# Expert stages of a six-stage kernel: on-chip slot inversion, a gather and a scatter per block, a norm by tile, shorter routing

## Chip, core and metric

One core of a Trainium2 chip runs the whole kernel in one launch. The metric is the device time of that core in microseconds (us), lower is better. Engines: PE (TensorE), DVE (VectorE), ACT (ScalarE), POOL (GpSimd), SP (SyncE, which issues DMAs).

## What is computed

x has 1024 tokens of 256 features. Six stages follow one another, "fafmsm": expert layer with 2 experts (f), attention (a), f again, expert layer with 8 experts (m), a state-space mixer (s), m again. Each starts with a layer norm of x and adds its result to x.

```python
x = x + 0.5 * _L0_ffn_ref(_layernorm(x), ...)   # 2 experts, the best one counts
x = x + _L0_attn_ref(_layernorm(x), ...)
x = x + 0.5 * _L0_ffn_ref(_layernorm(x), ...)
x = x + 0.5 * _L1_ffn_ref(_layernorm(x), ...)   # 8 experts, the best two count
x = x + _L1_attn_ref(_layernorm(x), ...)        # mixer
x = x + 0.5 * _L1_ffn_ref(_layernorm(x), ...)

# f: probs = softmax(x @ gate_w.T); sel = argmax; y = (silu(x Wg) * (x Wu)) Wd of expert sel, times probs[sel]
# m: probs = softmax(gelu(x @ rw1) @ rw2); top 2; for each expert e and rank k:
#      Ye = gelu(x w1[e] + b1[e]) w2[e] + b2[e];  Ce = gelu(b1[e]) w2[e] + b2[e]
#      out += active * wgt[k] * (Ye where idx[k] == e, else Ce)
```

## The kernel before

**Tiles.** x stays in SBUF as 8 tiles of 128 tokens (X). Matrices are held as two float16 parts (high and low), and a product is three matmuls: high by high, high by low, low by high.

**An expert stage** (`moe_stage`, stages 1, 3, 4, 6) has these steps.
- Norm (`layernorm_stage`): DVE waits for all of x, then runs statistics (L121), aggregation (L124), epsilon (L126), the root on ACT (L142), reciprocal (L128) and the normalised rows XN (L130), each for all eight tiles. Then PE turns each tile (L153), ACT makes the high half XTh (L145), DVE the low half XTl (L134), two PSUM banks in turn.
- Router: PE (L362; L373 and L378 with 8 experts), DVE from L551 on: softmax, masks, rank by rank.
- Slots: tokens are sorted by expert into blocks of 128 rows. PE counts (L387, L390), DVE computes a slot for each token (L578 to L591) and the expert of each block (L593 to L596).
- Rows: POOL scatters the rows of XN to their slots in DRAM (L683, one indirect DMA for each tile and rank: 8 with one expert a token, 16 with two). SP then loads whole blocks (L704).
- With 8 experts, DVE also makes coefficients (L600 to L611), PE turns them (L398), ACT copies them (L506); in stage 4 the bias product follows (L777, 192 matmuls; L794 on DVE).
- Blocks: NB0 = 9 with 2 experts, NB1 = 23 with 8. In step b PE runs turn_h(b) (L441), first(b+1) (L430), turn_x(b+2) (L412) and second(b) (L457). DVE copies the result (L640), SP stores it (L708). SP's order is load(b+3), store(b).
- Return: once all blocks are stored, POOL gathers each token's rows (L694), four buffers, and DVE adds them to X (L666), and with 8 experts the bias part (L671).

**Other stages.** Attention (stage 2) has its own norm and adds its result at L1206, in the order of tiles 0, 4, 1, 5 and so on. The mixer (stage 5) loads constants by SP once x is there, DVE starts with L1674, and adds its result at L1738. Each engine's program is the stages' programs one after another, so an engine reaches the next stage only when it has issued all of this one.

**Weights.** In stage 1 three matrices are split in two halves by ACT (L259) and DVE (L264), then the attention weights (L191, L201). POOL splits the matrix w1 in 17 chunks (L216, L201), 14 of them between its scatters and its gathers of stage 1, the other 3 at the start of attention. Then it splits w2 in 20 chunks to DRAM (L1226, L1228). Stage 4 loads w2 back (L760, 8 MB), stage 6 again.

Of the kernel before, what the change touches and what calls it, by code (L numbers as in the profile page):

```python
# [19 lines left out]
P = 128  # L20
# [14 lines left out]
EPS = 1e-5  # L35

# [69 lines left out]
def layernorm_stage(c, x_done, x_count, XN):  # L106

    s_var = c.sem("ln_var", 1)
    s_sd = c.sem("ln_sd", 1)
# [5 lines left out]
    stats, mv, veps, sd, rstd = c.ln_stats, c.ln_mv, c.ln_veps, c.ln_sd, c.ln_rstd  # L115

    def dve(eng):
        link = c.dve_link
        eng.wait_ge(*x_done(x_count))
        for t in range(NT):  # L120
            ins = eng.bn_stats(stats[:, t, :], X[:, t, :])  # L121
        link(ins)
        for t in range(NT):
            ins = eng.bn_aggr(mv[:, t, :], stats[:, t, :])  # L124
        link(ins)
        eng.tensor_scalar(veps[:, :], mv[:, :, 1], EPS, None, ALU.add).then_inc(s_var.sem, 1)  # L126
        eng.wait_ge(*s_sd(1))
        link(eng.reciprocal(rstd[:, :], sd[:, :]))  # L128
        for t in range(NT):
            eng.tensor_scalar(XN[:, t, :], X[:, t, :], mv[:, t, 0:1], rstd[:, t:t + 1],  # L130
                              ALU.subtract, ALU.mult).then_inc(s_xn.sem, 1)
        for t in range(NT):
            eng.wait_ge(*s_hi(t + 1))
            eng.tensor_tensor(XTl[:, :, t * P:(t + 1) * P], pst(t), XTh[:, :, t * P:(t + 1) * P],  # L134
                              ALU.subtract).then_inc(s_lo.sem, 1)

    def pst(t):
        return c.bank(6 + t % 2)[:, 0:D].rearrange("p (k t) -> p k t", k=KD)

    def act(eng):  # L140
        eng.wait_ge(*s_var(1))
        eng.activation(sd[:, :], veps[:, :], ACT.Sqrt).then_inc(s_sd.sem, 1)  # L142
        for t in range(NT):
            eng.wait_ge(*s_tps(t + 1))
            eng.activation(XTh[:, :, t * P:(t + 1) * P], pst(t), ACT.Copy).then_inc(s_hi.sem, 1)  # L145

    def pe(eng):
        for t in range(NT):
            eng.wait_ge(*s_xn(t + 1))
            if t >= 2:  # L150
                eng.wait_ge(*s_lo(t - 1))
            for k in range(KD):
                ins = eng.transpose(pst(t)[:, k, :], XN[:, t, k * P:(k + 1) * P], c.ident[:, :])  # L153
            ins.then_inc(s_tps.sem, 1)
# [1933 lines left out]
```

## Time and profile before

| | us |
|---|---|
| median of 3 runs (lowest, highest) | 1248.28 (1246.53, 1250.77) |
| profiled execution, own time | 1248.47 |
| its span, first to last instruction | 1246.9 |
| PE busy | 910.6 (73%) |
| DVE, ACT, POOL busy | 558.5, 350.2, 383.0 |

The page gives busy time by engine, the chain of work that ended last, and groups of instructions by line. A "granted clock" is TensorE's, as a share of full speed. In the timeline a row has the start in us, the duration in us, the engine, the line, the operation, output <- input, the count and, in brackets, how long the engine was idle before it and what ended that.

### The profile page before, as it was taken

To read this page: it belongs to the slowest core of one execution; us is meant where nothing else is said; L and a number is where in the kernel's file an instruction comes from. 1 tells how busy PE (TensorE), PEld (TensorE's weight loads), DVE (VectorE), ACT (ScalarE), POOL (GpSimd) and SP (SyncE) were. 2 spreads that over 40 slices of the span, in tenths; PEclk is the share of its full clock that TensorE was granted. 3 is DMA by queue.
4 is the path that set the end of the run, shared out by engine and by line. 5 is a ranking of instruction groups with operands and counts; after the bars stand their busy time and mean duration, and the time that the engine had idled before them with its cause. 6 is when DMAs were issued, how large, how long until landed. Compare 5 with 4: busy or idle time off the path is not lost.

```text
span 1246.9 us, 18377 instructions
## 1 busy us (share of the span) xinstructions
PE 910.6 (73%) x5986; PEld 516.2 (41%) x5987; DVE 558.5 (45%) x1090; ACT 350.2 (28%) x594; POOL 383.0 (31%) x360
## 2 busy tenths in 40 slices
PE   2199625498887279924899999568699744999993
PEld 1056412122223136612556666334244431666661
DVE  5523373567772423354023333365699550332333
ACT  3322111155553122211033333136211221333330
POOL 0695167888100100033100000413798313000004
PEclk9999957599998579965899999769999966999996
DMA  8453127555100010053101111230000152111103
GB/s 306 149 150 93 37 83 239 186 172 180 52 15 2 22 38 26 22 198 155 43 27 34 42 34 34 65 125 1 1 0 1 34 251 70 34 38 37 34 30 106
DMA packets 47576, 98.63 MB, mean 79 GB/s; under 512 B 10208, under 2 KB 32240, under 8 KB 46624
## 3 DMA queue, kind: packets, MB, share of 16 engines
q1 hardware_dynamic: 36400, 57.09, 13.1%
q0 software_dynamic: 11120, 40.77, 10.4%
q8 instruction: 38, 0.62, 0.2%
q14 instruction: 18, 0.15, 0.0%
HBM read 65.97 MB, written 31.85 MB: 78 GB/s over the span
## 4 chain that ended last, share of the span: by engine, by line
PE 65%; DVE 13%; issue 6%; DMA 5%; POOL 5%; ACT 3%; SPq 2%; DVEq 0%; POOLq 0%; ACTq 0%
PE psum L430 19%; PE psum L457 14%; PE psum L1057 6%; PE psum L441 4%; POOL xg_dram L683 3%; PE psum L1515 3%; PE psum L425 2%; POOL mem L694 2%; PE psum L777 2%; PE psum L1032 2%; DVE mem L130 2%; DVE mem L1151 1%; PE psum L1462 1%; PE psum L412 1%; DMA mem<-yg_dram,mem 1%
## 5 line engine op out<-in xcount | busy, mean ns | idle before, releaser
L430 PE MATMUL psum<-mem 128*128 x984 | 240.8, 391 | 0.4 <-issue 0.3
L694 POOL DMA_INDIRECT mem<-yg_dram,mem x48 | 46.0, 958 | 514.8 <-DMA yg_dram<-mem 501.4
L457 PE MATMUL psum<-mem 128*128 x1536 | 178.2, 273 | 4.7 <-DVE mem L632 4.7
L457 PEld LDWEIGHTS psum<-mem 128*128 128x128 f16 x1536 | 149.9, 98 | 23.3 <-issue 5.6
L430 PEld LDWEIGHTS psum<-mem 128*128 128x128 f16 x984 | 90.9, 100 | 119.2 <-issue 33.9
L683 POOL DMA_INDIRECT xg_dram<-mem x48 | 56.6, 1180 | 211.5 <-DVE mem L591 198.1
L1151 DVE TENSOR_REDUCE mem<-psum 128x2 f32<-128x1024 f32 (+2 forms) x96 | 89.4, 951 | 59.5 <-PE psum L1010 37.6
L1109 ACT ACTIVATE mem<-psum 128x512 f32<-128x512 f32 (+1 forms) x160 | 80.0, 552 | 106.2 <-PE psum L1040 66.2
L632 DVE TENSOR_TENSOR mem<-psum,mem 128x512 f16<-128x512 f32 x128 | 82.5, 686 | 49.8 <-ACT mem L525 49.8
L525 ACT ACTIVATE mem<-psum 128x512 f16<-128x512 f32 x128 | 69.5, 595 | 124.4 <-PE psum L441 124.4
L153 PE MATMUL psum<-ident,mem 128*128 128x128 f32 x96 | 26.8, 430 | 97.3 <-DVE mem L130 78.0
L1057 PE MATMUL psum<-mem 128*17 128x512 f32 (+3 forms) x384 | 81.5, 521 | 17.2 <-DVE mem L1170 17.2
L620 DVE COPY mem<-mem 16x128 f16 (+1 forms) x46 | 9.9, 216 | 166.2 <-ACT mem L513 166.2
L520 ACT ACTIVATE mem<-psum 128x1024 f32<-128x1024 f32 x46 | 47.1, 1023 | 130.9 <-PE psum L430 130.9
L412 PE MATMUL psum<-ident,mem 128*128 128x128 f32 x128 | 26.2, 288 | 65.5 <-DMA mem<-xg_dram 60.7
L441 PE MATMUL psum<-ident,mem 128*128 128x128 f32 x512 | 66.6, 273 | 7.0 <-DVE mem L627 4.7
L627 DVE TENSOR_TENSOR mem<-mem,psum 128x1024 f32<-128x1024 f32 x18 | 22.0, 1221 | 94.6 <-ACT mem L518 94.6
L1515 PE MATMUL psum<-mem 128*128 128x512 f32 x112 | 53.7, 603 | 11.9 <-DVE psum L1722 11.4
L441 PEld LDWEIGHTS psum<-ident,mem 128*128 128x128 f32 x512 | 57.7, 141 | 9.7 <-DVE mem L627 5.7
L153 PEld LDWEIGHTS psum<-ident,mem 128*128 128x128 f32 x96 | 14.9, 205 | 108.5 <-DVE mem L130 81.3
L640 DVE COPY mem<-psum 128x256 f32<-128x256 f32 x64 | 27.2, 425 | 64.0 <-PE psum L457 64.0
L412 PEld LDWEIGHTS psum<-ident,mem 128*128 128x128 f32 x128 | 17.9, 147 | 78.5 <-issue 66.9
(228 smaller groups left out, 1368.3 us busy)
## 6 DMA issues: line engine op xcount, KB each, us to landing
stage<-in_w POOLq DMA_DIRECT2D x20, 480.0 KB, 5.2
mem<-xg_dram SPq DMA_DIRECT2D x64, 128.0 KB, 2.0
stage<-in_w POOLq DMA_DIRECT2D x16, 512.0 KB, 3.9
yg_dram<-mem SPq DMA_DIRECT2D x64, 128.0 KB, 1.7
w2h_dram<-mem POOLq DMA_DIRECT2D x20, 240.0 KB, 2.8
w2l_dram<-mem POOLq DMA_DIRECT2D x20, 240.0 KB, 3.6
mem<-w2h_dram SPq DMA_DIRECT2D x2, 2048.0 KB, 11.8
mem<-w2l_dram SPq DMA_DIRECT2D x2, 2048.0 KB, 16.9
```

The lines of the kernel that those rows point to most:

```text
L412: ins = eng.transpose(c.bank(7)[:, k * P:(k + 1) * P], xg[:, p, k * P:(k + 1) * P], c.ident[:, :])
L430: ins = eng.matmul(out, a[:, p, k, :], w[:, at], start=(i == 0), stop=(i == last))
L441: ins = eng.transpose(c.bank(4 + q)[:, j * P:(j + 1) * P], h[:, p, (q * half + j) * P:(q * half + j + 1) * P], c.ident[:, :])
L457: ins = eng.matmul(c.bank(6)[:, 0:D], a[:, q * half + j, :], w[:, at], start=(i == 0), stop=(i == 3 * CF - 1))
L525: eng.activation(hTh[:, q * 4:q * 4 + 4, :], c.bank(4 + q).rearrange("p (j t) -> p j t", j=4), ACT.Copy)\
L632: eng.tensor_tensor(hTl[:, q * 4:q * 4 + 4, :], c.bank(4 + q).rearrange("p (j t) -> p j t", j=4), hTh[:, q * 4:q * 4 + 4, :], ALU.subtract ...
L683: eng.indirect_dma_start(c.xg_dram[0:NB * P, :], bass.IndirectOffsetOnAxis(ap=sloti[:, k, t:t + 1], axis=0), XN[:, t, :], None).then_inc(s ...
L694: eng.indirect_dma_start(yg[:, g % NYG, :], None, c.yg_dram[0:NB * P, :], bass.IndirectOffsetOnAxis(ap=sloti[:, k, t:t + 1], axis=0)).then ...
L1057: ins = eng.matmul(out, va[:, k, 2 * p + j, :], pt[:, (p * NS + i) % RING, j, off:off + w], start=(k == 0), stop=last)
L1109: eng.activation(pt[:, (p * NS + i) % RING, j, 0:w], c.bank(4 + (at + j) % 3)[:, 0:w], ACT.Exp, scale=DK ** -0.5).then_inc(s_ex.sem, 1)
L1151: eng.tensor_reduce(out, c.banks(2 * (i % 2), 2).rearrange("p (j q) -> p j q", j=2)[:, :, 0:w], AX.X, ALU.max)\
L1515: ins = eng.matmul(acc(2 * p + j), gm[:, i % RING, j, :], xw[:, i % RING, j, :], start=False, stop=True, skip_group_check=True)
```

## The change

- **Slots inverted on chip.** For each tile and rank, `oh` is a one-hot of the slot's place in its block (128 wide) and `idb` the token's row number at the slot's block, zero elsewhere. PE sums their products into bank 3: a table of which row each slot holds. It gives `idx` for gathers and `yidx` for scatters; unused slots read a row of zeros and write to spare rows.
- **Rows.** SP stores each tile of XN to DRAM as it is made (once for each rank), in token order. POOL gathers block b's rows by `idx` and scatters its result by `yidx`, both indirect DMAs, in the order gather(b+2), (chunks of w1 in stage 1), scatter(b). After the last block SP loads each tile's results with a plain DMA.
- **Norm.** Runs tile by tile: DVE's loop takes one tile's addition of results (`combine`), the aggregation of the tile before, statistics, the low half of the tile two before and XN of the tile before. Root and reciprocal are one addition and one power on POOL.
- **Combination** of a stage's results moves to the next stage's norm loop (or to the end of the kernel). The bias part is added for all tiles before that.
- **Routing** works on differences of logits, with fewer DVE steps; softmax sums are taken later; counts come first on PE.
- **w1.** One or two chunks stand between gather(b+2) and scatter(b); the last 3 follow attention's norm on POOL.
- **Bias product of stage 4:** 256 matmuls of 2 columns with w2 as the stationary side, then a sum and a turn, in place of 192 of 256 columns. Its input is made by POOL, not DVE.
- PE's, ACT's and the rest of DVE's work in the blocks is as before.

```diff
 def layernorm_stage(c, src, XN):
     def dve(eng):
-        eng.wait_ge(*x_done(x_count))
-        (statistics, aggregation, epsilon, reciprocal, XN for t in range(NT), then all low halves)
+        for i in range(NT + 2):
+            if i < NT and combine:
+                combine[0](eng, i)
+            if 1 <= i <= NT:
+                t = order[i - 1]
+                eng.wait_ge(*s_st(i))
+                eng.bn_aggr(mv[:, t, :], stats[:, t, :]).then_inc(s_ag.sem, 1)
+            if i < NT:
+                t = order[i]
+                for part in combine[1:]:
+                    part(eng, i)
+                eng.wait_ge(*ready(i))
+                eng.bn_stats(stats[:, t, :], X[:, t, :]).then_inc(s_st.sem, 1)
+            if i >= 2:
+                eng.wait_ge(*s_hi(i - 1))
+                eng.tensor_tensor(XTl[:, :, tok(order[i - 2])], pst(i - 2), XTh[:, :, tok(order[i - 2])],
+                                  ALU.subtract).then_inc(s_lo.sem, 1)
+            if 1 <= i <= NT:
+                t = order[i - 1]
+                eng.wait_ge(*s_rs(i))
+                eng.tensor_scalar(XN[:, t, :], X[:, t, :], mv[:, t, 0:1], rstd[:, t:t + 1],
+                                  ALU.subtract, ALU.mult).then_inc(s_xn.sem, 1)
+    def pool(eng):
+        for i, t in enumerate(order):
+            eng.wait_ge(*s_ag(i + 1))
+            eng.tensor_tensor(rstd[:, t:t + 1], mv[:, t, 1:2], c.ln_consts[:, 0:1], ALU.add).then_inc(s_ve.sem, 1)
+            eng.wait_ge(*s_ve(i + 1))
+            eng.tensor_tensor(rstd[:, t:t + 1], rstd[:, t:t + 1], c.ln_consts[:, 1:2], ALU.pow).then_inc(s_rs.sem, 1)
...
 def moe_stage(...):
     def pe(eng):
...
+        eng.wait_ge(*s_idb(1))
+        for i in range(KT):
+            eng.wait_ge(*s_oh(i + 1))
+            ins = eng.matmul(c.bank(3)[:, 0:NB], oh[:, i, :], idb[:, i, :], start=(i == 0), stop=(i == KT - 1))
+        ins.then_inc(s_ids.sem, 1)
...
     def dve(eng):
...
+        for i in range(KT):
+            eng.tensor_scalar(oh[:, i, :], c.iota_p[:, :], pcol[:, i // NT, i % NT:i % NT + 1], None, ALU.is_equal)\
+                .then_inc(s_oh.sem, 1)
...
+    def combine_first(eng, t):
+        eng.wait_ge(*s_yg[t](16))
+        if not gated:
+            eng.wait_ge(*s_bts(t + 1))
+        ins = eng.scalar_tensor_tensor(c.X[:, t, :], yg[t][:, 0, :], wkh[:, 0, t:t + 1], c.X[:, t, :], ALU.mult, ALU.add)
+        ins.then_inc(s_xd.sem if TOPK == 1 else s_add.sem, 1)
...
     def pool(eng):
-        (16 or 8 scatters of XN; the w1 chunks; gathers of the results)
+        def gather(b):
+            if b >= 2:
+                eng.wait_ge(*s_xt(b - 1))
+            eng.indirect_dma_start(xg[:, b % 2, :], None, c.xn_dram[0:T * TOPK + 1, :],
+                                   bass.IndirectOffsetOnAxis(ap=idx[:, b:b + 1], axis=0)).then_inc(s_xg[b % 2].sem, 16)
+        def scatter(b):
+            eng.wait_ge(*s_yo(b + 1))
+            eng.indirect_dma_start(c.y_dram[:, :], bass.IndirectOffsetOnAxis(ap=yidx[:, b:b + 1], axis=0),
+                                   yo[:, b % 2, :], None).then_inc(s_ys[b % 2].sem, 16)
+        gather(0)
+        gather(1)
+        eng.wait_ge(*s_yi(1))
+        for b in range(NB):
+            if b + 2 < NB:
+                gather(b + 2)
+            if meanwhile is not None:
+                meanwhile(eng, b)
+            scatter(b)
     def sync(eng):
-        (loads and stores of blocks in turn)
+        for i, t in enumerate(order):
+            eng.wait_ge(*L["xn"](i + 1))
             for k in range(TOPK):
+                row = 1 + k * T + t * P
+                eng.dma_start(c.xn_dram[row:row + P, :], XN[:, t, :]).then_inc(s_xs.sem, 16)
+        if weights_sync is not None:
+            weights_sync(eng)
         for p in range(2):
             eng.wait_ge(*s_ys[p](16 * ((NB + 1 - p) // 2)))
+        rows = c.y_dram[1:1 + T * TOPK, :].rearrange("(k t p) d -> t p k d", k=TOPK, t=NT)
         for t in range(NT):
+            eng.dma_start(yg[t], rows[t]).then_inc(s_yg[t].sem, 16)
```

## Rows read from the trace of the kernel before

**Rows 1.** The page, section 4: the chain that ended last, by engine.
```profile
PE 65%; DVE 13%; issue 6%; DMA 5%; POOL 5%; ACT 3%; SPq 2%; DVEq 0%; POOLq 0%; ACTq 0%
```
**Rows 2.** Busy time by window, blocks of stage 4 and the mixer; engines, clock, DMA.
```profile
621.40:789.50 168.10, 165.82 (x1101) 107.68 (x1101) 50.96 (x113) 55.55 (x91) 0.00 (x0) 0.99 0.11 33
827.90:993.80 165.90, 139.82 (x494) 69.85 (x494) 117.16 (x121) 51.12 (x80) 101.06 (x99) 0.95 0.00 1
```
**Rows 3.** Timeline, start of the third stage, from the logits to the first rows.
```profile
421.96 0.17 DVE L551 TENSOR_REDUCE mem<-psum 128x8 f32<-128x16 f32 x1 [1.60 <-PE psum L362]
...
428.45 1.05 POOL L683 DMA_INDIRECT xg_dram<-mem  x1 [108.39 <-DVE mem L591]
...
441.91 0.66 PE L412 MATMUL psum<-ident,mem 128*128 128x128 f32 x2 [16.03 <-DMA mem<-xg_dram]
```
**Rows 4.** Pieces of the chain that ended last: start us, us, what.
```profile
22.15 1.44 PE psum L362 x48
...
437.39 2.39 DMA xg_dram<-mem
...
542.80 2.74 DMA mem<-yg_dram,mem
```
**Rows 5.** Timeline, the norm of the third stage.
```profile
407.75 2.71 DVE L121 BATCH_NORM_STATS2 ln_stats<-X 128x6 f32<-128x256 f32 x8
...
418.39 1.09 PE L153 MATMUL psum<-ident,mem 128*128 128x128 f32 x4 [0.60 <-DVE XTl L134]
...
419.50 0.85 DVE L134 TENSOR_TENSOR XTl<-psum,XTh 128x256 f16<-128x256 f32 x2 [0.83 <-ACT XTh L145]
```
**Rows 6.** Timeline, start of the fourth stage: logits and first block.
```profile
566.38 0.23 DVE L551 TENSOR_REDUCE mem<-psum 128x8 f32<-128x64 f32 x1 [5.60 <-PE psum L378]
...
618.83 0.44 PE L412 MATMUL psum<-ident,mem 128*128 128x128 f32 x2 [0.51 <-DVE mem L794]
```
**Rows 7.** Timeline, one block of the sixth stage.
```profile
1126.73 1.04 PE L441 MATMUL psum<-ident,mem 128*128 128x128 f32 x8
...
1127.04 0.42 DVE L640 COPY mem<-psum 128x256 f32<-128x256 f32 x1 [0.96 <-PE psum L457]
...
1131.04 0.38 PE L412 MATMUL psum<-ident,mem 128*128 128x128 f32 x2
...
1134.19 0.42 DVE L640 COPY mem<-psum 128x256 f32<-128x256 f32 x1 [0.96 <-PE psum L457]
```
**Rows 8.** Timeline, first stage: a w1 chunk, the last blocks, the next norm.
```profile
66.58 2.13 POOL L201 TENSOR_TENSOR mem<-stage,mem 128x1024 f16<-128x1024 f32 x1
...
141.00 0.42 DVE L640 COPY mem<-psum 128x256 f32<-128x256 f32 x1 [0.34 <-PE psum L457]
...
145.86 0.42 DVE L640 COPY mem<-psum 128x256 f32<-128x256 f32 x1 [2.51 <-PE psum L457]
...
166.82 8.26 DVE L130 TENSOR_SCALAR mem<-X,ln_mv,ln_rstd 128x256 f32<-128x256 f32 x8
```
**Rows 9.** The mixer's power on POOL: count, ns min/median/max, first and last start.
```profile
L1810 POOL TENSOR_TENSOR mem<-mem x8: 548/548/572, 923.5 to 987.7; 128x1 f32<-128x1 f32 x8
```
**Rows 10.** Timeline, end of the kernel: last block, first and last additions.
```profile
1217.35 0.42 DVE L640 COPY mem<-psum 128x256 f32<-128x256 f32 x1 [2.50 <-PE psum L457]
...
1222.52 0.49 DVE L666 SCALAR_TENSOR_TENSOR X<-mem,X 128x256 f32<-128x256 f32 x1 [4.75 <-DMA mem<-yg_dram,mem]
...
1241.84 0.42 DVE L671 SCALAR_TENSOR_TENSOR X<-psum,X 128x256 f32<-128x256 f32 x1
```
**Rows 11.** Timeline, start of the mixer.
```profile
828.38 1.89 POOL L1772 TENSOR_TENSOR stage<-stage,mem 128x1024 f32<-128x1024 f32 x1 [16.09 <-DMA mem<-in_mix_norm]
...
830.78 0.69 DVE L1674 TENSOR_TENSOR mem<-psum,mem 128x512 f32<-128x512 f32 x1 [2.97 <-PE psum L1447]
```
**Rows 12.** Timeline, start of the sixth stage: logits and first block.
```profile
1011.07 0.23 DVE L551 TENSOR_REDUCE mem<-psum 128x8 f32<-128x64 f32 x1 [4.66 <-PE psum L378]
...
1046.71 0.66 PE L412 MATMUL psum<-ident,mem 128*128 128x128 f32 x2 [16.24 <-DMA mem<-xg_dram]
```

More of the change, by code:

```diff
@@ new lines, in pool, with pst @@
+    def pool(eng):
[4 more added lines that the diff above has]
+            eng.tensor_tensor(rstd[:, t:t + 1], rstd[:, t:t + 1], c.ln_consts[:, 1:2], ALU.pow).then_inc(s_rs.sem, 1)
+    def pst(i):
+        return c.bank(6 + i % 2)[:, 0:D].rearrange("p (k t) -> p k t", k=KD)
+    def act(eng):
+        for i in range(NT):
+            eng.wait_ge(*s_tps(i + 1))
+            eng.activation(XTh[:, :, tok(order[i])], pst(i), ACT.Copy).then_inc(s_hi.sem, 1)
@@ L147, in pe @@
     def pe(eng):
[L148 to L151, printed above, removed]
+        for i in range(NT):
+            eng.wait_ge(*s_xn(i + 1))
+            if i >= 2:
+                eng.wait_ge(*s_lo(i - 1))
             for k in range(KD):
-                ins = eng.transpose(pst(t)[:, k, :], XN[:, t, k * P:(k + 1) * P], c.ident[:, :])
+                ins = eng.transpose(pst(i)[:, k, :], XN[:, order[i], k * P:(k + 1) * P], c.ident[:, :])
@@ L301, in moe_stage @@
     xgl = region.take([2, KD, P], F16)
+    at = region.at
     h = region.take([2, FF], F32)
+    end = region.at
+    region.at = at
+    oh = region.take([KT, P], F16)
+    eqb = region.take([KT, NB], F32)
+    idb = region.take([KT, NB], F16)
+    region.at = end
     hTh = region.take([CF, P], F16)
@@ L355, in pe @@
         if gated:
-            eng.wait_ge(*L["lo"](NT))
-            for t in range(NT):
+            for n, t in enumerate(order):
+                eng.wait_ge(*L["lo"](n + 1))
                 tok = slice(t * P, (t + 1) * P)
@@ L1250, in attention_stage @@
     return dict(pe=pe, act=act, dve=dve, pool=pool, sync=sync, done=s_xd, count=NT,
+                order=[t + HALF * h for t in range(HALF) for h in range(2)], ready=lambda i: s_xd(i + 1), combine=[],
                 w2_stored=[s_ws[p](16 * CHUNKS) for p in range(2)])
@@ L1298, in level_units, with mixer_stage @@
     return out
-def mixer_stage(c, x_done, x_count, A, region, region2, stage, after):
+def mixer_stage(c, src, A, region, region2, stage, after):
     n = lambda name, total: c.sem("mix_" + name, total)
@@ L1822, in pool @@
                 todo[what](t)
-    return dict(pe=pe, act=act, dve=dve, pool=pool, sync=sync, done=s_xd, count=NT)
+    return dict(pe=pe, act=act, dve=dve, pool=pool, sync=sync, done=s_xd, count=NT,
+                order=list(range(NT)), ready=lambda i: s_xd(i + 1), combine=[])
 def mixer_layouts(v):
@@ L2022, in _ @@
                         g["dve"](eng)
+                for t in range(NT):
+                    for part in st["combine"]:
+                        part(eng, t)
             @block.tensor
             def _(eng):
-                eng.wait_ge(*s_z(3))
+                eng.wait_ge(*s_z(5))
                 eng.wait_ge(*s_const(64))
```

498 lines of the change are left out of this document (249 added, 249 removed).

## Prediction

> **What bounds the kernel now.** I read the page first: TensorE holds 65% of the chain that ended last, and in each window of expert blocks it is busy nearly throughout [rows 1, 2]. So the change, which touches no block arithmetic, can gain only in the stretches between block loops, and can lose only where a block starts to wait. Then I read the timeline at each of those stretches, and last one block in steady state.
>
> Between loops four things stand on the path. The slots are known at the first scatter (428.45), but TensorE gets rows only at 441.91: eight scatters 1.28 us apart ((437.39 - 428.45)/7), 2.39 us until the last lands, then 2.13 us for the plain load and the wake (441.91 - 437.39 - 2.39) [rows 3, 4]. After the last block a store and 8 or 16 gathers bring results back at 1.26 us each, 2.74 us from the start of one to its landing [rows 4]. Then the norm: 12.6 us, 407.75 to 420.35 [rows 5]. In the fourth stage the bias product holds TensorE until 618.83, released by VectorE's L794, not by rows [rows 6].
>
> Inside an 8-expert block (7.15 us, L640 to L640) the row load is hidden. I take t0 = 1126.73 (turn_h). The previous block's result is copied at t0 + 0.73, and turn_x two blocks ahead starts at t0 + 4.31 [rows 7].
>
> **Part 1: a gather per block, on GpSimd's queue.** The matmuls, their order and their waits stay. What changes is the order of issue. SyncE issued load(b+3) before store(b); GpSimd now issues gather(b+2) after scatter(b-1), and scatter(b-1) waits for the result of block b-1. So gather(b+2) can't start before that result, and everything behind the waiting scatter on GpSimd waits too. Path: copy ends (0), GpSimd wakes 0.28 (the gap from L591 to L683), scatter 1.26 to 1.28, gather 2.74, TensorE wakes 0.14: 4.42 us [rows 3, 4]. From t0 + 0.73 this gives t0 + 5.15 against a need at t0 + 4.31: late by 0.84 us in the first block it hits. Now it is a loop: turn_x, second, copy, scatter, gather, turn_x. From turn_x to the end of the copy is 1134.61 - 1131.04 = 3.57 us, and 0.22 more because starved transposes aren't overlapped (0.44 for two at 618.83, 0.22 in flow) [rows 6, 7]. Period 4.42 + 3.79 = 8.21 us in place of 7.15: +1.06 us. It holds for 20 of the 23 blocks (gather(0) to gather(2) come early, the last two steps turn no rows). **Two stages: 20 x 1.06 x 2 = +42 us.** Bounds: +0.76 a step if transposes stay overlapped and the end of second is as at a stage's last block, +1.4 if the gather takes 0.3 longer: +30 to +56.
>
> In the 2-expert stages a block is 8.9 us, because it has two first matmuls; the same arithmetic leaves about 0.8 us of slack, so nothing in the third stage.
>
> The Trainium skill ("DMA: Bandwidth & Descriptors", Anatomy of one DMA, the SWDGE path) fits a GpSimd DMA by 2.0 us plus bytes over 436 GB/s, which for 128 KB is an estimate of 2.30 us against the 2.74 of the row. By the page the period would be 7.77, this part +25 and the whole 1218; no run of the kernel before shows a gather behind a scatter, so the nearest row decides and the sum goes by it.
>
> **Part 2: stage 1, with the w1 split on the same queue.** A chunk costs GpSimd 4.11 us (L201 2.13, the cast before it 1.05, the issue 0.56, gaps) [rows 8]. Blocks with two chunks need 8.2 + 2.5 = 10.7 us of GpSimd in a block of 8.9, so gather(4), (6) and (8) come about 1.2 us late: +3.6. The last scatter stands behind two chunks that began after scatter(7), while the last block takes only 145.86 - 141.00 = 4.86 us: about 5.8 us late. Against that: the start of the blocks stays held by the split of the attention weights (within 1 us of now), and the norm of stage 2 loses its collision with GpSimd (eight L130 in 8.26 us, 2.67 where GpSimd is idle) [rows 8]. Three chunks now run beside the mask and memset work behind it, +2 (0 to +6). The end of stage 2's norm comes at 179.1 instead of 180.9, its constants at 180.2. **Together +1 (-3 to +6).**
>
> **Part 3: the norm by tile.** One tile's loop: normalise ends, transposes and high half 1.25 (0.14, and 418.39 to 419.50), low half 0.43, normalise 0.41: 2.07 us, serial, because the low half of tile i-2 and the normalise of tile i-1 alternate. GpSimd's two operations (0.55 for the power, 0.19 to 0.63 for the addition, two wakes) hide beside the statistics and the low half [rows 5, 9]. Where x isn't combined by this code (after attention, after the mixer) VectorE reaches it only after its last addition, since its stream is in order: 2.1 + 7 x 2.07 + 1.66 = 18.2 us against 12.6, **+5.6 each.** Where results are combined, VectorE's own work (1.85 us with one gathered row, 2.4 with two) fills the loop: 2.15 and 2.4 us per tile.
>
> **Part 4: return path.** The last scatter adds 0.28 + 2.39, SyncE's plain loads 2.1: the first tile is there 4.8 us after the copy, as the first gather's is now (1222.52 - 1217.77) [rows 10]. After it: 19.8 us to the end of the norm with one row; now 9.3 for eight gathers, 12.6 for the norm and, at the end of the third stage, 2.1 that the normalise loses to GpSimd's split of b1: **-4.3**, counted in part 6. With two rows (fourth stage): the norm is done at about 817, some 10 earlier. But VectorE's L1674 also waits for the mixer's constants, which are asked for when the last x is done and land at 828.2; they move with it, by 2 us: start 826.3 for 830.78 [rows 11]: **-4.5.** At the end: after the last copy (1217.77) two additions a tile, 1.02 us: 8 tiles done at about 1231.3 for 1242.26 [rows 10]: **-11** (-9 if 256 KB a tile loads slower than 1.02 us).
>
> **Part 5: routing.** VectorE before the masks: 5 operations for 12 (2 experts), 11 for 18 (8 experts), 0.205 and 0.257 us each: -1.4 and -1.9. After: rounding, 8 or 16 one-hots, the product, the copy. No row shows a one-hot of 128 columns; between 0.14 and 0.23 each (0.23 is the cast of 128 columns), I take 0.17 as most are back to back: 6.4 us from L551 to the first DMA with 2 experts, where rows show 6.49 [rows 3]; 12.1 with 8 against 12.0. **0 (-1.5 to +1.5 a stage).**
>
> **Part 6: scatters gone at each start.** Third stage: the gather lands 2.88 us after it starts, not 13.46: -10.6; last logits no longer behind all low halves -0.8; norm +5.6: **-5.8.** Sixth stage: indices at L551 + 11.8; then VectorE makes coef (about 18 operations, 4.1 us), TensorE turns it (3.6), ScalarE copies it (1.1) before the first turn_x, at L551 + 20.7. Now 1046.71 - 1011.07 = 35.6 [rows 12]. -14.9, norm +5.6: **-9.3.** Fourth stage: L551 at 562.1 instead of 566.38 (part 4); indices 573.9; coef turned 581.5; then the new bias product. It has 256 matmuls of 2 columns; 48 of that kind take 1.44 us (0.03 each) [rows 4], so 7.7, and I take 10 for instruction gaps (8 to 16); then 1.5 for the sum and the turn: turn_x at 593 for 618.83: **-26** (-30 to -20), the -4.3 inside [rows 6]. The xn stores stand behind the w2 loads on SyncE's queue here, landing at about 582: hidden by the bias product; without it +8.
>
> **Sum.** 42 + 1 - 4.5 - 11 - 5.8 - 9.3 - 26 = -13.6 us. The profiled execution took 1248.47 (span 1246.9), 0.2 from the median 1248.28: **1235 us.** With the bounds, 1221 to 1253.
>
> **The rivals.**
> - *The gather is in time* (or only part of it is late). Then parts 2 to 6 are left: -56, 1193; half late, 1214. For it: in 2-expert blocks there is slack, and the loss rests on 0.84 us. Against it: every term has a row, and the order of the queue leaves no other way.
> - *Slower: starved TensorE loses its clock.* The loops now run at a granted 0.99 with TensorE 98.6% busy; the mixer, 84% busy, has 0.95 [rows 2]. The new loops would be 87% busy. A block with TensorE at its lower level (1.2 GHz) would take some 13 us instead of 8.2 (twice the 7 us of matmuls, less the slack), so each point below 0.99 (2% of 43 blocks) costs about 4 us. Up to 0.96 it stays inside my range; below about 0.955 it is slower than before; at 0.93, 1259.
> - *The path isn't shortened on chip:* one-hots at 0.23 and GpSimd's product of 16 x 23 columns behind VectorE's use of the shared memory path, 3 us more at each of the four starts, and the stage-1 queue at its upper bound: 1252, no change.
>
> **How the numbers follow.** Forecast (0.84 or more late a block, clock kept) 0.68, spread over 1221 to 1253; gather in time or partly 0.17; clock 0.08; starts not shortened 0.07. For eight in ten: from 1197 (0.1 of the first rival left out below) to 1255 (0.05 of the clock's and 0.04 of the forecast's tail left out above). A change under 0.3% (3.7 us) can't be told from none here. Faster needs under 1244.5: the first rival, and 0.57 of the forecast's 0.68: 0.74. Within 0.3% (1244.5 to 1252): 0.06 of the forecast and 0.06 of the third rival, 0.12. Slower: 0.05 of the forecast, the clock's 0.08, 0.01 of the third: 0.14.
>
> **What would show it.** Period of the block in the 8-expert loops: 8.2 right, 7.2 wrong; and if 8.2, L412 waits for the gather into xg. In the 2-expert loop of stage 3: 8.9. Norm after attention 18 us, at the end of the kernel 8 tiles in 8.3 us. First turn_x of the fourth stage about 31 us after L551 (52 now). The prediction falls if the gather's flight behind a scatter isn't 2.74, or if GpSimd wakes late at each wait.

## The result, and the profile after

| | median of runs, us | profiled span, us | mean granted clock |
|---|---|---|---|
| before | 1247.85 (1246.53 to 1250.77) | 1246.9 | 0.867 |
| after | 1266.46 (1264.21 to 1271.98) | 1264.5 | 0.879 |

The medians are of four runs each. The ratio is 1.0145, with a 95% interval of 1.0113 to 1.0177: the change makes the kernel 1.5% slower. The forecast was 1235, with 1197 to 1255 as its range.

VectorE's copy of each block's result (128x256 out of PSUM; L640 before, L707 after) cuts the span into pieces that can be laid side by side. The third column is what my parts gave for the piece.

| piece, us | before | after | difference | forecast |
|---|---|---|---|---|
| start to first copy | 78.98 | 75.11 | -3.9 | 0 |
| loop of stage 1, first to last copy | 66.88 | 75.34 | +8.5 | +3.6 |
| to the first copy of stage 3 | 318.84 | 307.33 | -11.5 | -8.4 |
| loop of stage 3 | 66.88 | 67.37 | +0.5 | 0 |
| to the first copy of stage 4 | 103.11 | 75.05 | -28.1 | -26 |
| loop of stage 4 | 154.75 | 197.35 | +42.6 | +21.2 |
| to the first copy of stage 6 | 273.16 | 252.75 | -20.4 | -13.8 |
| loop of stage 6 | 154.75 | 197.48 | +42.7 | +21.2 |
| last copy to the end | 29.55 | 16.72 | -12.8 | -11 |

Outside the loops the change gained 76.7 us where I had 59.2. Inside them it lost 94.3 where I had 46. The two 8-expert loops are the case: +85.3 against +42.

The page of the kernel after, section 4 (chain by engine) and two groups of section 5. The chain by engine answers to [rows 1]:

```profile
PE 46%; DMA 17%; DVE 15%; issue 8%; POOL 8%; ACT 4%; SPq 1%; DVEq 0%; POOLq 0%; ACTq 0%
...
L768 POOL DMA_INDIRECT y_dram<-mem x64 | 63.7, 995 | 430.1 <-DVE mem L707 420.6
L515 PE MATMUL psum<-mem 128*128 x1536 | 189.2, 282 | 28.0 <-issue 23.3
```

TensorE fell from 65% to 46% of the chain; DMA rose from 5% to 17%. Ahead of its scatters (L768) GpSimd stood idle 420.6 us, waiting for VectorE's copies. The third line is the one to remember: before L515, the matmuls of the second layer, TensorE sat idle for 28.0 us, 23.3 of them "issue", waiting for nothing that the profile shows.

Windows of the kernel after, the loop of stage 4 and the mixer (us, then busy time and count of PE, PEld, DVE, ACT, POOL; granted clock; DMA share; GB/s). They answer to [rows 2]:

```profile
587.10:797.80 210.70, 177.01 (x1101) 106.73 (x1102) 51.10 (x113) 57.59 (x91) 41.22 (x42) 0.98 0.09 27
831.00:990.00 159.00, 132.08 (x435) 64.81 (x432) 117.51 (x121) 48.60 (x78) 101.00 (x99) 0.98 0.00 1
```

The loop took 42.6 us more, TensorE was busy 11.2 us more in it (177.01 against 165.82), and the granted clock went from 0.99 to 0.98: 31 us of the 42.6 are idle time.

One block of stage 6 in the timeline of the kernel after, weight loads left out; it answers to [rows 7]:

```profile
1186.05 0.43 DVE L707 COPY mem<-psum 128x256 f32<-128x256 f32 x1 [2.28 <-PE psum L515]
...
1186.75 0.99 POOL L768 DMA_INDIRECT y_dram<-mem  x1 [6.48 <-DVE mem L707]
...
1188.05 0.97 POOL L763 DMA_INDIRECT mem<-xn_dram,mem  x1 [0.30 <-issue]
...
1190.93 0.43 PE L470 MATMUL psum<-ident,mem 128*128 128x128 f32 x2 [0.71 <-DMA mem<-xn_dram,mem]
...
1192.04 2.81 PE L515 MATMUL psum<-mem 128*128 x24 [0.68 <-issue]
...
1194.99 0.42 DVE L707 COPY mem<-psum 128x256 f32<-128x256 f32 x1 [2.52 <-PE psum L515]
```

This is the cycle of part 1 in my order: copy ends 1186.48, scatter 0.27 later, gather 1.30 after that, 2.76 of flight and 0.12 until the transposes (L470). That makes 4.45, for which I had 4.42. Then come 1.11 us from the transposes' start to the second layer's, 2.95 to the copy and 0.42 for it: 4.48, for which I had 3.79. The period is 8.94 in this block, and 8.7 to 9.1 in most. The 1.11 isn't the same in all: it alternates between about 0.87 and 1.09, with a mean of 0.97 over the 40 blocks that wait.

### The profile page after: what moved, and what is told of

The parts are those of the page before. It is cut to its first block, busy times and chain, and to the rows that moved or that the text cites. A ratio compares the mean times of both kernels' runs of the same rounds, so it can differ in the third digit from the quotient of the medians.

```text
span 1264.5 us, 18377 instructions
## 1 busy us (share of the span) xinstructions
PE 926.1 (73%) x6132; PEld 505.6 (40%) x6133; DVE 559.4 (44%) x1097; ACT 344.1 (27%) x581; POOL 453.1 (36%) x494
## 3 DMA queue, kind: packets, MB, share of 16 engines
q1 hardware_dynamic: 28578, 49.98, 11.2%
## 4 chain that ended last, share of the span: by engine, by line
PE 46%; DMA 17%; DVE 15%; issue 8%; POOL 8%; ACT 4%; SPq 1%; DVEq 0%; POOLq 0%; ACTq 0%
PE psum L515 14%; DMA mem<-xn_dram,mem 11%; PE psum L488 6%; PE psum L1137 5%; POOL y_dram L768 4%; PE psum L1597 3%; PE psum L172 2%; PE psum L470 2%; PE psum L1112 2%; DVE mem L1231 2%; POOL mem L220 2%; DVE mem L707 2%; DMA max_dram<-mem 2%; DVE XTl L143 1%; PE psum L1624 1%
## 5 line engine op out<-in xcount | busy, mean ns | idle before, releaser
L488 PE MATMUL psum<-mem 128*128 x984 | 239.3, 390 | 0.5 <-issue 0.4
L768 POOL DMA_INDIRECT y_dram<-mem x64 | 63.7, 995 | 430.1 <-DVE mem L707 420.6
L515 PE MATMUL psum<-mem 128*128 x1536 | 189.2, 282 | 28.0 <-issue 23.3
L515 PEld LDWEIGHTS psum<-mem 128*128 128x128 f16 x1536 | 151.0, 101 | 62.3 <-issue 39.3
L172 PE MATMUL psum<-ident,mem 128*128 128x128 f32 x96 | 32.5, 441 | 95.2 <-DVE mem L148 95.2
L1137 PE MATMUL psum<-mem 128*17 128x512 f32 (+3 forms) x384 | 84.4, 538 | 16.9 <-DVE mem L1250 16.9
L763 POOL DMA_INDIRECT mem<-xn_dram,mem x64 | 69.0, 1078 | 61.0 <-issue 35.0
L707 DVE COPY mem<-psum 128x256 f32<-128x256 f32 x64 | 27.2, 425 | 137.5 <-PE psum L515 137.5
L470 PE MATMUL psum<-ident,mem 128*128 128x128 f32 x128 | 29.0, 311 | 76.9 <-DMA mem<-xn_dram,mem 47.2
L499 PE MATMUL psum<-ident,mem 128*128 128x128 f32 x512 | 66.6, 273 | 7.0 <-DVE mem L694 4.7
L154 POOL TENSOR_TENSOR ln_rstd<-ln_mv,ln_consts 128x1 f32<-128x1 f32 x48 | 10.6, 221 | 158.0 <-DVE ln_mv L134 158.0
L1597 PE MATMUL psum<-mem 128*128 128x512 f32 x112 | 53.7, 603 | 11.9 <-DVE psum L1804 10.2
L499 PEld LDWEIGHTS psum<-ident,mem 128*128 128x128 f32 x512 | 57.7, 141 | 9.7 <-DVE mem L694 5.7
L172 PEld LDWEIGHTS psum<-ident,mem 128*128 128x128 f32 x96 | 13.7, 201 | 112.9 <-DVE mem L148 105.6
```

The source lines that it names most:

```text
L172: ins = eng.transpose(pst(i)[:, k, :], XN[:, order[i], k * P:(k + 1) * P], c.ident[:, :])
L488: ins = eng.matmul(out, a[:, p, k, :], w[:, at], start=(i == 0), stop=(i == last))
L499: ins = eng.transpose(c.bank(4 + q)[:, j * P:(j + 1) * P], h[:, p, (q * half + j) * P:(q * half + j + 1) * P], c.ident[:, :])
L515: ins = eng.matmul(c.bank(6)[:, 0:D], a[:, q * half + j, :], w[:, at], start=(i == 0), stop=(i == 3 * CF - 1))
L763: eng.indirect_dma_start(xg[:, b % 2, :], None, c.xn_dram[0:T * TOPK + 1, :], bass.IndirectOffsetOnAxis(ap=idx[:, b:b + 1], axis=0)).then_ ...
L768: eng.indirect_dma_start(c.y_dram[:, :], bass.IndirectOffsetOnAxis(ap=yidx[:, b:b + 1], axis=0), yo[:, b % 2, :], None).then_inc(s_ys[b % ...
```

## The experiments

**e1: the gathers one block earlier.**

```diff
         gather(1)
+        gather(2)
         eng.wait_ge(*s_yi(1))
         for b in range(NB):
-            if b + 2 < NB:
-                gather(b + 2)
+            if b + 3 < NB:
+                gather(b + 3)
```

> Theory Q (the place in GpSimd's queue): in the changed kernel the gather of block b+2 stands behind the scatter of block b-1, which waits for the end of that block, and it is needed 3.8 us after that end. Here each gather is issued one block earlier (gather(0), (1), (2), then gather(b+3) ahead of scatter(b)), so it has a whole block of slack; everything else is as in the changed kernel. Q expects the waits on the gather to go in all loops, the two loops of 23 blocks to be 168 us each again (7.15 us a block, within 3) instead of 210.7 and 211.2, the first stage 2 to 4 us shorter, and the whole near 1178 us (1170 to 1186), faster than the kernel before. Rival F (the indirect transfers themselves: two of them from one queue in a block, their flights stretching each other): the loops stay above 185 us each and the whole above 1215. Rival C (TensorE's clock level, seen as 4.4 us second layers in place of 2.8): the loops are near 175 us each and 1190 to 1200 in all.

Measured: 1170.39 us, ratio to before 0.9368 (0.9331 to 0.9404). A block of stage 6 in its timeline, and its window for stage 4:

```profile
1049.15 0.42 DVE L707 COPY mem<-psum 128x256 f32<-128x256 f32 x1 [0.96 <-PE psum L515]
...
1049.85 0.99 POOL L768 DMA_INDIRECT y_dram<-mem  x1 [4.89 <-DVE mem L707]
...
1051.15 0.97 POOL L763 DMA_INDIRECT mem<-xn_dram,mem  x1 [0.30 <-issue]
...
1053.16 0.38 PE L470 MATMUL psum<-ident,mem 128*128 128x128 f32 x2
```

```profile
577.70:745.70 168.00, 165.72 (x1103) 107.91 (x1103) 51.34 (x113) 55.45 (x91) 41.10 (x42) 0.99 0.11 33
```

GpSimd's two lines stand at the same distance behind the copy as in the slow kernel, 0.70 and 2.00 us. What changed is which block the gather is for: the transposes at 1053.16 wait for nothing, because their rows were asked for a block before. Both 8-expert loops are 154.75 us from first to last copy, just as before the change. Stage 1's is 66.88, 8.5 us shorter where I had 2 to 4. The time is at the low end of what I expected (1170 to 1186). Rivals F and C fall. The whole loss of the loops hung on one place in a queue; the kernel is 96 us faster than the one as changed.

**e2: the register load ahead of the wait.**

```diff
             first(b + 1, 1 - p)
+            e = load_e(b)
             if x:
                 turn_x(b + 2, p)
-            second(b, p, first_use)
+            second(b, p, first_use, e)
```

> In the changed kernel TensorE stands idle 0.43 to 0.68 us between the transposes of a late gather and the first matmul of the second layer, which my sum did not have. Theory V: this is the register load of the block's expert number, which stands in the program behind the wait for the gather and so is done late. Here it is moved ahead of that wait; nothing else changes. V expects the gap to go, 0.4 to 0.7 us a block over about 20 blocks of two loops, so 1240 to 1250 us against 1266. Rival W (the gap is the engine's start after a starved wait, whatever stands there): no change, 1264 to 1269.

Measured: 1231.49 us, ratio 0.9854 (0.9814 to 0.9893). Timeline of a block of stage 6, and the group of the second layer on its page:

```profile
1155.21 0.43 PE L470 MATMUL psum<-ident,mem 128*128 128x128 f32 x2 [0.77 <-DMA mem<-xn_dram,mem]
...
1155.48 2.78 PE L519 MATMUL psum<-mem 128*128 x24
```

```profile
L519 PE MATMUL psum<-mem 128*128 x1536 | 181.8, 276 | 4.7 <-DVE mem L704 4.7
```

The gather is as late as ever, but the second layer now starts 0.27 us after the transposes in place of 1.11, and the idle time before it is 4.7 us in place of 28.0. Theory V holds and W falls, at 35 us and not 16 to 26. In the two 8-expert loops it is 33.5 us. Of these, 26.5 (the top of what I expected) are the earlier start of the second layer: over the 40 blocks the mean from the transposes' start is 0.31 us for 0.97, because the idle time and the lost overlap of the transposes with the matmuls behind them both go. The other 7 aren't the load itself: in the changed kernel five second layers took 4.34 to 4.47 us instead of 2.81, here only one took longer (4.12); the granted clock had fallen in them (see the rivals below). The common period is 8.12 us, close to the 8.21 of my part 1.

**e3: the wait without the scatter.** The results go back in slot order, by a plain store of SyncE, so the rows that return belong to other tokens, and the later stages route other values.

```diff
         def scatter(b):
             eng.wait_ge(*s_yo(b + 1))
-            eng.indirect_dma_start(c.y_dram[:, :], ..., yo[:, b % 2, :], None).then_inc(s_ys[b % 2].sem, 16)
     def sync(eng):
+        for b in range(NB):
+            eng.wait_ge(*s_yo(b + 1))
+            eng.dma_start(c.y_dram[1 + b * P:1 + (b + 1) * P, :], yo[:, b % 2, :]).then_inc(s_ys[b % 2].sem, 16)
```

> The scatter is left out; GpSimd still waits for the block's result before it issues the next gather, and SyncE stores the result with a plain transfer in slot order (so the output is not the reference's: the rows that return are those of other tokens). Theory Q with my terms: the chain from the copy's end to the transposes loses just the scatter's issue, 1.30 us a block over about 20 blocks of two loops, so both loops drop from 211 to about 185 us and the whole to about 1212 us (1205 to 1220). Rival F (the scatter's transfer slows the gather's flight, 2.7 us alone and 3.5 in clusters): more than that, the flights fall to 2.7 or below everywhere and the whole is under 1200. Rival H (what counts is the wait alone, the issue runs beside it): over 1245.

Measured: 1189.92 us, ratio 0.9518 (0.9478 to 0.9557), 76 us less than the changed kernel where I had 54 (71 us in the profiled spans). Timeline of a block:

```profile
1101.95 0.42 DVE L707 COPY mem<-psum 128x256 f32<-128x256 f32 x1 [1.39 <-PE psum L515]
...
1102.65 0.94 POOL L763 DMA_INDIRECT mem<-xn_dram,mem  x1 [6.64 <-DVE mem L707]
...
1105.96 0.38 PE L470 MATMUL psum<-ident,mem 128*128 128x128 f32 x2
...
1106.46 2.82 PE L515 MATMUL psum<-mem 128*128 x24
```

The gather starts 0.70 us after the copy starts, instead of 2.00: just the scatter's 1.30. Most blocks that had periods of 8.7 to 9.1 us now have 7.3 to 7.8. The two loops lost 59.9 us together (166.82 and 168.08), the loop of stage 1 another 6.7. Rival H falls. So the price has two parts: what stands between (the scatter), and the wait, which alone still costs some 0.4 us in such a block. In the block shown the rows are in time (the transposes follow the first layer without a gap), yet 0.50 us pass from the transposes to the second layer, for 0.22 before the change: the wait for the gather ends so late that the register load behind it isn't hidden.

The total lies in rival F's range (under 1200), but the flights don't: the long ones are still there, in the same places of the loop (3.53 to 3.70 us in stage 4, 3.46 to 3.65 in stage 6). F falls by them, not by the time. The 8 us beyond my 52 (40 blocks times 1.30) lie in the five blocks of 10.9 to 11.4 us, where no block takes over 9.2 here: they are the five with the long second layers, and this kernel has none.

**e5: empty slots on different rows.** The chain of the changed kernel shows the flights of the gathers. The first and the third of the loop of stage 4 (start, us), one from its middle, and three of its last four; below, two of the last four of stage 6:

```profile
602.21 2.83 DMA mem<-xn_dram,mem
...
619.77 3.64 DMA mem<-xn_dram,mem
...
684.33 2.74 DMA mem<-xn_dram,mem
...
747.67 3.62 DMA mem<-xn_dram,mem
...
766.97 3.86 DMA mem<-xn_dram,mem
776.77 3.60 DMA mem<-xn_dram,mem
...
1217.41 3.62 DMA mem<-xn_dram,mem
1226.97 3.54 DMA mem<-xn_dram,mem
```

In e2 the long ones belong to the same blocks, though the last of them run 13 and 32 us earlier there. A block's empty slots hold index 0, so they all read row 0. On top of e2 (the last line is cut at the dots):

```diff
-        eng.tensor_copy(idx[:, :], c.bank(3)[:, 0:NB]).then_inc(s_idx.sem, 1)
+        link(eng.tensor_scalar(spare[:, :], c.bank(3)[:, 0:NB], 0.0, None, ALU.is_equal))
+        eng.scalar_tensor_tensor(idx[:, :], spare[:, :], c.row_ids[:, 0:1], c.bank(3)[:, 0:NB], ALU.mult, ALU.add)...
```

> In the changed kernel and in e2 the gathers that land late (3.5 to 3.9 us in place of 2.7 to 2.9) are those of the same blocks each time: the third in the loop, one in the middle of the sixth stage, and the last four of both stages. Theory R: these blocks hold empty slots, all of which read one row of the normalized rows (row 0), and many reads of one address are slow. Here, on top of e2, empty slots read 128 different rows (partition p reads row 1 + p; their results go to spare rows as before, so the output is the reference's). R expects every flight at 2.7 to 2.9 us, every period near 8.12, both loops near 174 us from first to last copy (e2: 182.0 and 179.3), so 11 to 15 us less than e2: 1216 to 1221. Rival D (what else the DMA engines carry at those times, or the place in the stage): the same flights stay above 3.4 and the time stays at 1228 to 1234.

Measured: 1217.26 us, ratio 0.9816 (0.9794 to 0.9837). This set's runs of the kernel before had a median of 1241.56, e2's 1249.87, so the two ratios can't be told apart (their intervals overlap) and the traces have to decide. The chain of this kernel, the last two flights of stage 4 and the last of stage 6, and windows over most of both loops:

```profile
744.85 2.70 DMA mem<-xn_dram,mem
752.86 2.76 DMA mem<-xn_dram,mem
...
1181.39 2.69 DMA mem<-xn_dram,mem
```

```profile
597.00:753.00 156.00, 141.27 (x917) 86.96 (x914) 43.52 (x97) 47.32 (x76) 37.41 (x40) 1.00 0.10 32
1026.00:1180.00 154.00, 140.80 (x914) 86.82 (x912) 42.94 (x95) 47.37 (x77) 37.21 (x38) 1.00 0.10 33
```

All 40 flights on the chain now take 2.69 to 2.86 us, the periods are 7.8 to 8.5 but for one of 8.95, and the loops are 175.20 and 173.70 us (e2: 181.96 and 179.33), 12.4 us less together. Theory R holds as far as row 0 goes; D falls. Whether it is the many reads of one address, or something about row 0 itself, isn't separated. The windows bear on the clock as well: TensorE starves in every block here, 91% busy, at a granted 1.00.

**e4: the norm in passes again, after attention and the mixer** (on top of e1).

```diff
+        if batch:
+            (statistics of 8 tiles, aggregates of 8, wait for GpSimd's one addition and one power,
+             8 normalisations, 8 low halves)
+            return
```

> The kernel of e1 with the layer norms at the starts of the third and sixth stages (after attention and after the mixer) done in passes over all eight tiles again: statistics of all, one addition and one power on GpSimd for all, then all normalizations. The norm by tile took 17 us of chain after attention and the old norm 12.6; expected 4 to 5 us less at each of the two starts, so 8 to 10 us less than e1. Rival: the tile-wise form hid the stores of the normalized rows and the first half of the router behind its later tiles, which now come at once at the end; then the gain is 0 to 3 us in all.

Measured: 1168.51 us, ratio 0.9348 (0.9309 to 0.9387); 1.9 us less than e1 in the medians, 2.5 in the spans. The norm after attention, in e4 and then in the kernel after:

```profile
402.25 2.70 DVE L133 BATCH_NORM_STATS2 ln_stats<-X 128x6 f32<-128x256 f32 x8
...
407.70 2.67 DVE L141 TENSOR_SCALAR mem<-X,ln_mv,ln_rstd 128x256 f32<-128x256 f32 x8 [2.08 <-POOL ln_rstd L176]
...
415.34 0.85 DVE L145 TENSOR_TENSOR XTl<-psum,XTh 128x256 f16<-128x256 f32 x2 [0.83 <-ACT XTh L190]
```

```profile
408.99 0.42 DVE L140 BATCH_NORM_STATS2 ln_stats<-X 128x6 f32<-128x256 f32 x1
...
425.53 0.42 DVE L143 TENSOR_TENSOR XTl<-psum,XTh 128x256 f16<-128x256 f32 x1 [1.20 <-ACT XTh L164]
```

In passes it takes 13.9 us (402.25 to 416.19), by tile 17.0 (408.99 to 425.95): 3.0 less, not 4 to 5, as the passes wait 2.08 us for GpSimd's two operations; the old norm, whose root ran on ScalarE, took 12.6 in all [rows 5]. From the last copy to the next first copy e4 is 2.5 us shorter than e1 at the third stage and 1.4 at the sixth. Together 3.9 us, not 8 to 10: the forecast failed, and the sum is close to the rival's 0 to 3. But the rival's reason isn't what the rows show: the norm itself gained only 3.0, and 2.5 of them reach the start of the third stage. A ratio can't show it.

**e6: the w1 chunks behind the scatter** (on top of e4).

```diff
+            scatter(b)
             if meanwhile is not None:
                 meanwhile(eng, b)
-            scatter(b)
```

> The kernel of e4, with the w1 chunks of the first stage issued behind the scatter of their block on GpSimd's queue instead of ahead of it. With gathers a block ahead the chunks cost the loop nothing in e1 (66.88 us from the first to the last copy, as before the change), but the last scatter still stood behind chunks. Expected by my part 2: the last scatter goes at once after the last copy, some 5 to 6 us earlier; the two chunks then run beside the norm of the second stage and take 1 to 3 us of that back on GpSimd (its power and additions queue behind them: each chunk holds it 4.1 us, which could cost up to 8). Forecast 2 to 4 us less than e4, 1164 to 1167; rival: the first tile's norm waits for both chunks, and nothing is gained or 2 to 4 us lost, 1168 to 1173.

Measured: 1166.96 us, 1.6 less than e4; ratio 0.9425 (0.9389 to 0.9461), against other runs of the kernel before than e4's. GpSimd and SyncE around the end of stage 1, in e4 and then in e6:

```profile
148.87 1.02 POOL L794 DMA_INDIRECT y_dram<-mem  x1 [0.30 <-issue]
152.25 3.65 SPq L821 DMA_DIRECT2D mem<-y_dram  x8
155.81 0.18 POOL L180 TENSOR_TENSOR ln_rstd<-ln_mv,ln_consts 128x1 f32<-128x1 f32 x1 [5.92 <-DVE ln_mv L154]
```

```profile
147.81 1.04 POOL L794 DMA_INDIRECT y_dram<-mem  x1 [0.30 <-issue]
...
151.24 3.66 SPq L821 DMA_DIRECT2D mem<-y_dram  x8
...
157.16 0.20 POOL L180 TENSOR_TENSOR ln_rstd<-ln_mv,ln_consts 128x1 f32<-128x1 f32 x1
```

The last scatter comes 1.1 us earlier, not 5 to 6: the chunks of block 7 now stand ahead of scatter(8). The first addition of the next norm comes 1.35 us later, behind the chunks of block 8. One cancels the other, and from the last copy to the first of stage 3 the two kernels differ by 0.6 us. GpSimd has the same chunks to do in either order. The median is in my range (1164 to 1167), but not for my reason, and the ratio to the kernel before is higher than e4's.

**e7: e2's and e5's edits where nothing starves** (on top of e6).

> The kernel of e6 with the two edits that gained 35 and 14 us on the starved loops (the register load ahead of the wait, e2; empty slots on different rows, e5). If their gain came only from the chain that ran through the late gather, both are worth nothing here, where gathers are a block ahead: within 2 us of e6, 1163 to 1170, with periods of 7.15 as before; the added operation ahead of the indices may cost 0.2 us at each of four starts. Rival: they cost TensorE or the DMA engines something by themselves; then 5 us or more less than e6.

Measured: 1171.46 us, ratio 0.9398 (0.9374 to 0.9422), against e6's 0.9425 (0.9389 to 0.9461) and 4.5 us more in the medians; loops of 154.75 us again. The forecast was 1163 to 1170, and this set's kernel before had 1245.39 against 1241.56 in e6's, so no cost is shown either. What gained 33.5 and 12.4 us in the starved loops gains nothing off them. All kernels with the gathers a block ahead lie between 1167 and 1175 us, 6% under the kernel before.

**e8 and e9: what is late next at the start of the fourth stage.** On top of e7, e8 moves the coefficients' transposes and the bias product behind the last block; e9 also issues the w2 loads behind the stores of the normalised rows.

```diff
     (TensorE, 8-expert stages, ahead of the first block)
-            (transposes of coef); W["bias_pe"](eng); eng.wait_ge(*s_cfc(2))
     (behind the last block)
+            (transposes of coef); W["bias_pe"](eng); eng.wait_ge(*s_cfc(2))
     (e9, SyncE)
-    w2 loads; stores of XN
+    stores of XN; w2 loads
```

> The kernel of e7; in the two 8-expert stages the transposes of the coefficients and the bias product (fourth stage only) are moved from ahead of the first block to behind the last one, where TensorE waits for the results' return anyway. My part 6 said what is late next at the start of the fourth stage: the stores of the normalized rows, which stand behind the w2 loads on SyncE's queue (in the changed kernel gather(0) starts 10.7 us after the indices, at 577.70, and would release TensorE at 580.6, bias at 584.0). So expected here: the fourth stage starts 3 to 4 us earlier, not 17; the sixth 2 to 5 us earlier (there TensorE waited for the coefficients at 1033.7 and the gathers could be there at 1028.5 if the stores let them). Together 1158 to 1163. Rival: the stores aren't in the way and both starts follow the indices; then 1146 to 1152. Other rival: the work shows at the stages' ends, no change.

> The kernel of e8 with the loads of w2 issued behind the stores of the normalized rows on SyncE's queue, in the fourth and in the sixth stage. If the stores are what is late next (e8's first theory), gather(0) now starts with the indices, and the first transposes follow them by some 3.5 us: the fourth stage starts another 8 to 10 us earlier than in e8, the sixth 0 to 5, together 1146 to 1154. Rival: w2, now asked for 3 to 4 us later, lands later than the first block needs it and takes the place of the stores: 0 to 4 us less than e8.

Measured: e8 1174.81 us, 0.942 (0.9392 to 0.9448), e9 1173.89 us, 0.9414 (0.9387 to 0.944): neither differs from e7. My totals were 1158 to 1163 and 1146 to 1154. The timelines show why: first the first transposes of the fourth stage in the kernel after; then those of e8 with two rows of its stage end, and last the first transposes of e9:

```profile
584.00 0.69 PE L470 MATMUL psum<-ident,mem 128*128 128x128 f32 x2 [0.50 <-DVE mem L875]
```

```profile
571.76 0.66 PE L490 MATMUL psum<-ident,mem 128*128 128x128 f32 x2 [14.52 <-DMA mem<-xn_dram,mem]
...
746.93 4.25 SPq L828 DMA_DIRECT2D mem<-y_dram  x8
...
755.73 0.76 DVE L765 SCALAR_TENSOR_TENSOR X<-psum,X 128x256 f32<-128x256 f32 x2 [2.23 <-PE psum L577]
```

```profile
569.76 0.66 PE L490 MATMUL psum<-ident,mem 128*128 128x128 f32 x2 [12.66 <-DMA mem<-w2l_dram]
```

The releaser goes from the bias product (VectorE's L875) to the gather behind the stores, and with the stores out of the way to the w2 load. From the last copy of stage 3 to the first of stage 4 it is 75.32 us in e7, 72.38 in e8, 69.52 in e9: 3 us a step, as the first theory of e8 and the rival of e9 had it. But on the way to the sixth stage e8 gives back 5.3 us and e9 8.7: in e8 the additions of the bias (L765) start 11.9 us after the last copy (743.79), where e7's start 1.05 after it, and the combines stand behind them. So e8's other rival, that the work shows at the ends, is true beside its first theory. Why e9 gives back 3.4 us more than e8 isn't separated. Both are also 2 us longer than e7 on the way from stage 1 to stage 3, where these edits change nothing: differences of that size are noise.

## Why the prediction was wrong

**Part 1, mechanism right, size wrong: the step that failed.** That gather(b+2) can't start before the result of block b-1, and that this makes a loop through the second layer, is what e1 and e3 show. The term of the sum that failed is "0.22 more because starved transposes aren't overlapped", which allowed 0.44 us from the transposes' start to the second layer's. It was 0.97 in the mean. Means over the 40 blocks of the two loops that wait for a late gather, in us, from the copy's end to the next copy's end:

| | forecast | before | after | e2 | e5 | e3 |
|---|---|---|---|---|---|---|
| copy's end to transposes | 4.42 | 3.59 | 4.74 | 4.75 | 4.48 | 3.73 |
| transposes to second layer | 0.44 | 0.22 | 0.97 | 0.31 | 0.30 | 0.68 |
| second layer to copy's end | 3.35 | 3.34 | 3.57 | 3.38 | 3.35 | 3.36 |
| period | 8.21 | 7.15 | 9.28 | 8.44 | 8.13 | 7.78 |

The 85.3 us that the loops lost are 40 times 2.13, and the three rows divide them. The first is 46.0 us for 33.6: the common blocks have 4.4 to 4.5, as I had, and what is beyond comes mostly from flights of blocks with empty slots, 10.6 us that e5 takes back. The second is 30.1 us for 8.8. Between transposes and second layer TensorE's queue holds a register load. In the kernel before it ran ahead, beside the first layer's matmuls (in the block of [rows 7] the trace has it at 1128.14, 2.9 us ahead of the transposes), so I hadn't costed it. In the block of the changed kernel shown above it starts at 1191.06, behind the transposes. There it is paid in each block, and e2 gets 26.5 us back by moving it. The third is 9.2 us for nothing: five second layers at a fallen clock.

So the register load is the largest miss, 21 us, and e2 shows it: without it the change is faster than the kernel before (0.9854), with it slower (1.0145). Flights and clock are the others, and e5, without all three, has 39.4 us over the kernel before (348.90 - 309.50) against my +42. My upper bound of +56 took in a longer flight, not a second cost that starvation uncovers, so the range fell with the term. I had asked of TensorE what its matmuls do when they starve, and not what its other instructions do.

The fit of the Trainium skill ("DMA: Bandwidth & Descriptors", Anatomy of one DMA, the SWDGE path) makes an estimate of 2.30 us for 128 KB. The flights of e5 take 2.69 to 2.86, so the row (2.74) was the better guide and the measurement decides.

**The rivals.** *In time* fell: no block of the 8-expert loops that turns rows behind such a gather escaped. *Starts not shortened* fell. *The clock* doesn't explain the loss, since e5's loops starve at 1.00, but it has a share that my sum put at nothing. In five of the 40 blocks the granted clock fell and the second layer took 4.34 to 4.47 us instead of 2.81: 8 us of the 85.3, and these are the blocks of 10.9 to 11.4 us. One of them, and a window around another:

```profile
1073.51 0.43 PE L470 MATMUL psum<-ident,mem 128*128 128x128 f32 x2 [1.52 <-DMA mem<-xn_dram,mem]
1074.38 4.47 PE L515 MATMUL psum<-mem 128*128 x24 [0.43 <-issue]
```

```profile
620.00:632.00 12.00, 9.90 (x53) 5.70 (x52) 2.28 (x6) 2.49 (x4) 2.71 (x3) 0.86 0.11 33
```

In all five TensorE had stood idle for 1.4 us or more ahead of the transposes, behind a flight of over 3.5 us. But six other blocks of this kernel waited as long and kept their clock, and e2 has one fall in eleven such blocks. In e3, with shorter waits, and in e5 and e1 none falls. What decides between such blocks isn't shown.

**Part 2** was +1 for stage 1 and what follows. Three gathers in the loop cost 2.0, 2.0 and 4.4 us for my 1.2 each. In e5 they cost 1.3, 1.2 and 1.3: the misses of part 1 once more, with a second layer of 4.47 us in the third block. The last scatter began 5.9 us after the last copy's end (150.87, 156.78), for 5.8. The start was 3.9 earlier, which I had put at nothing and no run separates. From the kernel's start to the norm after attention the sum is +1.2 us (408.99 - 407.75). That this meets my +1 is luck: the start made up for the loop.

**Part 3:** 17.0 us for 18.2; an iteration is 1.94 for 2.07. Close, and e4 prices it at 3.0 against passes of this kernel.

**Part 4:** the end -12.8 for -11. Mixer's start: L1756 begins at 830.83, 33.3 us after the last copy, 41.3 before [rows 11]; -8.1 for -4.5, still released by the constants (L1756 waits for them), so their place was right and they came earlier than I had them. The mixer itself took 3.4 us less from there to its last result, which I had at nothing.

**Part 5:** near zero, as forecast: 6.6 us from the logits to the first DMA with 2 experts, for 6.4. The one-hots, which no row of the kernel before showed, took 0.24 us each (16 in 3.79), not 0.17; from the logits to the indices of the fourth stage it is 12.7 us for 11.8 (554.32 to 566.98).

**Part 6:** in the third stage 27.0 us from the norm's start to the first transposes, for 34.2 before (408.99 to 436.02): -7.1 for -5.8. Logits to first transposes in the fourth stage 29.7 us ("about 31"), in the sixth 21.1 (20.7); with the norm ahead of it the sixth start is 9.6 us shorter for 9.3. The new bias product took 8.5 us (574.12 to 582.62) for the 10 I had taken. The xn stores were hidden by it as I said: e8 shows them next. Taking them away is worth 3 us in e9 and not 8, as the w2 load comes next.

So parts 3 to 6 held, most with a gain somewhat larger than forecast, and part 2 came out by luck. In part 1 one term was 0.97 us where I had 0.44, forty times over, and taking its cause out (e2) turned the sign.

## What to carry to other kernels

When a transfer moves to a queue in which something waits for a block's result, write down for which block each issue is and when that block needs it; here each gather issued one block earlier, with the same two buffers, turned +1.5% into -6.3%. When a wait becomes late, cost everything that stands behind it in that engine's program, register loads and lost overlap too, since what used to run ahead is then paid each time. And where many padding slots fall into one transfer that something waits for, give each an address of its own: it was worth 12 us in the starved loops, and nothing where the gathers were ahead (e7).

## What the runs showed of the hardware

- A register load on TensorE behind a starved wait, with the overlap that goes with it, cost 0.66 us a block in the mean: 0.97 us from transposes to next matmul with it (changed kernel), 0.31 with it ahead of the wait (e2). With the rows in time it cost nothing (e7 against e6).
- In the two 8-expert loops, an indirect gather of 128 rows of 1 KB landed 2.69 to 2.86 us after its start when empty slots read different rows (e5), and in ten blocks 3.46 to 3.86 us when the empty slots all read row 0 (changed kernel); how many slots were empty in each wasn't counted.
- On GpSimd's queue an indirect issue followed a scatter after 1.28 us (scatters, [rows 3]) to 1.30 (a gather, changed kernel), and the first two gathers of the third stage stood 1.40 apart (432.97, 434.37).
- A loop in which TensorE was 91% busy and idle in every block kept a granted clock of 1.00 (e5). In the changed kernel, 84% busy in its loop of stage 4, five of 40 second layers took 4.34 to 4.47 us instead of 2.81, behind idle times of 1.4 us or more.
